# Plain fp32 products in place of split products in the output projection of a state-space attention part

## What is computed

```
proj = h @ W_in.T                       # gate (4096), hidden (4096), B and C (128 each), dt (64)
hidden, B, C = silu(conv4(...))         # causal convolution of 4 taps per channel, then silu
y = (chunked scan of C, B, dt*hidden) + D * hidden          # 64 heads of 64 channels, chunks of 32 tokens
yf = y * silu(gate)
yn = norm_w * (yf * rsqrt(mean(yf*yf) + 1e-5))
return yn @ W_out.T                     # 4096 -> 256: the output projection
```

## Time and profile before

| | us |
|---|---|
| median of 3 runs | 2118.07 |
| the three runs | 2114.32, 2118.07, 2148.47 |
| span of the profiled execution | 2145.4 |
| PE, DVE, ACT, POOL busy over the span | 1740.8, 1467.5, 1005.9, 1011.7 |

### The profile page before, as it was taken

How to read it: one execution, slowest core, us unless ns; L and a number is a source line. 1 busy time by engine, 2 the same in 40 slices (tenths; PEclk the granted TensorE clock), 3 DMA queues, 4 the chain that set the end, 5 groups by cost and what they waited for, 6 DMA issues and landing times. The chain is left out here.

```text
span 2145.4 us, 36030 instructions
## 1 busy us (share of the span) xinstructions
PE 1740.8 (81%) x9416; PEld 1471.1 (69%) x9416; DVE 1467.5 (68%) x2219; ACT 1005.9 (47%) x1824; POOL 1011.7 (47%) x938
## 2 busy tenths in 40 slices
PE   6699996899987999968999888604999999999400
PEld 5577775677775777756777666403999998999300
DVE  3589996699985899966999845512544556554344
ACT  3555553655554555536555432202655666555100
POOL 0445553455543455535555403885433444333576
PEclk8899998999998999989999966857555667555555
DMA  3022220122210222201222101224766777666233
GB/s 120 0 70 83 77 82 21 38 74 83 81 57 0 75 78 83 76 21 42 78 75 83 45 0 63 81 86 136 228 195 205 231 235 245 198 198 203 89 118 103
DMA packets 110563, 217.46 MB, mean 101 GB/s; under 512 B 14160, under 2 KB 51536, under 8 KB 110416
## 3 DMA queue, kind: packets, MB, share of 16 engines
q1 hardware_dynamic: 94928, 171.07, 25.2%
q0 software_dynamic: 15616, 46.15, 6.7%
HBM read 160.55 MB, written 56.62 MB: 101 GB/s over the span
## 5 line engine op out<-in xcount | busy, mean ns | idle before, releaser
L965 DVE SCALAR_TENSOR_TENSOR e<-bank,scal,e 128x511 f32<-128x511 f32 (+2 forms) x384 | 284.0, 740 | 36.6 <-DVE e L965 18.2
L436 PEld LDWEIGHTS bank<-m,xt 128*128 128x128 f32 x2048 | 243.4, 195 | 84.0 <-DVE xt L1006 83.8
L1288 POOL TENSOR_TENSOR ew_lo<-ew,ew_hi 128x352 fp32r<-128x352 f32 x160 | 152.4, 953 | 309.1 <-ACT ew_hi L695 309.1
L436 PE MATMUL bank<-m,xt 128*128 128x128 f32 x2048 | 267.6, 285 | 30.0 <-DVE xt L1006 29.7
L1301 POOL TENSOR_TENSOR ssq<-ssq,ysq 128x512 f32<-128x512 f32 x128 | 164.0, 1281 | 227.3 <-ACT ysq L753 227.3
L1288 POOL TENSOR_TENSOR wi_lo<-wi,wi_hi 128x512 fp32r<-128x512 f32 x128 | 219.2, 1713 | 51.3 <-ACT wi_hi L695 51.3
L368 PE MATMUL bank<-h_hi,wi_hi 128*128 x512 | 227.6, 445 | 17.0 <-POOL wi_lo L1288 14.6
L760 ACT ACTIVATE e<-e 128x512 f32<-128x512 f32 x128 | 81.0, 633 | 324.2 <-DVE e L965 324.1
L878 DVE TENSOR_TENSOR hid_lo_rows<-hid_rows,hid_hi_rows 88x256 fp32r<-88x256 f32 x160 | 67.4, 421 | 231.8 <-ACT hid_hi_rows L695 231.8
L368 PE MATMUL bank<-hw_hi,ew_hi 128*88 128x128 f32 x640 | 220.1, 345 | 0.4 <-POOL ew_lo L1288 0.2
L1000 DVE TENSOR_TENSOR m<-el,gmask 128x1024 f32<-128x1024 f32 x128 | 219.8, 1717 | 0.1
(11 more groups left out here) (247 smaller groups left out, 4436.4 us busy)
## 6 DMA issues: line engine op xcount, KB each, us to landing
ew<-expert_w SPq DMA_DIRECT2D x160, 432.0 KB, 3.8
wi<-in_w SPq DMA_DIRECT2D x128, 256.0 KB, 2.5
grouped<-zeros_out SPq DMA_DIRECT2D x64, 320.0 KB, 2.3
x_rows<-grouped POOLq DMA_DIRECT2D x80, 256.0 KB, 4.4
outputs<-y_rows SPq DMA_DIRECT2D x80, 256.0 KB, 4.4
wo<-out_w SPq DMA_DIRECT2D x128, 128.0 KB, 2.0
x_all<-x_t SPq DMA_DIRECT2D x4, 512.0 KB, 8.3
out_t<-x_all SPq DMA_DIRECT2D x4, 512.0 KB, 3.5
```

What stands on the lines that cost most here:

```text
L436: i = mm(p_y[:, t * P:(t + 1) * P], xt[:, t, hd * HEAD_DIM:hd * HEAD_DIM + P], m[:, t, hd, :], start=hd == 0, stop=hd == 1)
L965: v.scalar_tensor_tensor(dst[:, d:], src[:, 0:SEQ - d], taps(TAPS - 1 - d), dst[:, d:], ALU.mult, ALU.add).then_inc(S[done], 1)
L1288: return g_.tensor_tensor(dst, src, hi.bitcast(F32), ALU.subtract)
```

## The change

The output projection multiplies y itself with weights that carry the norm's weight, `wn = wo * norm_w`, in plain fp32. y_hi, y_lo, wo_hi and wo_lo with their instructions and semaphores are gone; wn stands where wo_hi stood on ACT. Since y is now read by PE itself, DVE waits before it overwrites a half of y until the out group that read it is done.

```diff
-            wo_hi = sb("wo_hi", [P, 2, EMB], F32R, on=part)
-            wo_lo = sb("wo_lo", [P, 2, EMB], F32R, on=part)
+            wn = sb("wn", [P, 2, EMB], on=part)
...
             def load_out(b, j, par):
-                sp.wait_ge(S["wo_lo"], START["wo_lo"] + b * PAIRS + j - 1)
+                sp.wait_ge(S["wn"], START["wn"] + b * PAIRS + j - 1)
...
                 if do_out:
-                    pe.wait_ge(S["y_lo"], g - 1)
-                    pe.wait_ge(S["wo_lo"], START["wo_lo"] + g - 1)
+                    pe.wait_ge(S["y_done"], START["y_done"] + g - 1)
+                    pe.wait_ge(S["wn"], START["wn"] + g - 1)
                     for k in range(KE):
-                        w = slice(k * P, (k + 1) * P)
-                        i = split_mm(p_out[k][:, :], wo_hi[:, par, w], wo_lo[:, par, w], y_hi[:, par, :], y_lo[:, par, :],
-                                     do_out == "first", do_out == "last")
+                        i = mm(p_out[k][:, :], wn[:, par, k * P:(k + 1) * P], y[:, par, :],
+                               start=do_out == "first", stop=do_out == "last")
...
-                if finish:
-                    act.wait_ge(S["y_done"], START["y_done"] + g - 1)
-                    act.wait_ge(S["out_mm"], START["out_mm"] + g - 3)
-                    f(y_hi[:, par, :], y[:, par, :], ACT.Identity, scale=scal[:, bass.ds(j - 2, 1), NW_AT:NW_AT + 1]
-                      .rearrange("p a n -> p (a n)")).then_inc(S["y_hi"], 1)
...
                 if finish:
+                    act.wait_ge(S["y_done"], START["y_done"] + g - 1)
                     act.wait_ge(S["ssq_done"], START["ssq_done"] + g - 2)
...
-                    high(wo_hi[:, q, :], wo[:, q, :]).then_inc(S["wo_hi"], 1)
+                    f(wn[:, q, :], wo[:, q, :], ACT.Identity, scale=scal[:, bass.ds(j - 1, 1), NW_AT:NW_AT + 1]
+                      .rearrange("p a n -> p (a n)")).then_inc(S["wn"], 1)
...
-                if finish:
-                    dve.wait_ge(S["y_hi"], START["y_hi"] + g - 1)
-                    dve.wait_ge(S["out_mm"], START["out_mm"] + g - 3)
-                    v.scalar_tensor_tensor(y_lo[:, par, :], y[:, par, :], col(j - 2, NW_AT), y_hi[:, par, :].bitcast(F32),
-                                           ALU.mult, ALU.subtract).then_inc(S["y_lo"], 1)
...
                     dve.wait_ge(S["y_sq"], START["y_sq"] + g - 2)
+                    dve.wait_ge(S["out_mm"], START["out_mm"] + g - 2)
                     v.tensor_tensor(y[:, q, :], yt[:, :], gs[:, q, :], ALU.mult).then_inc(S["y_done"], 1)
...
-                if take_out:
-                    pool.wait_ge(S["wo_hi"], g)
-                    low(wo_lo[:, 1 - par, :], wo[:, 1 - par, :], wo_hi[:, 1 - par, :]).then_inc(S["wo_lo"], 1)
```

More of the change, by code:

```diff
@@ L75, in sem @@
             return ctx.enter_context(nc.semaphore(name))
-        START = {"wi_lo": 2, "wo_lo": 2, "gate": 2, "y_done": 2, "out_mm": 2, "y_sq": 2, "y_hi": 2, "attn_res": 1,
+        START = {"wi_lo": 2, "wn": 2, "gate": 2, "y_done": 2, "out_mm": 2, "y_sq": 2, "attn_res": 1,
                  "taps": 1, "silu_g": 1, "xt_done": 1, "y_skip": 1, "ssq_done": 1, "ssm": 1,
@@ L231, in program @@
             ssq = sb("ssq", [P, SEQ], on=part)
-            acc, xf, gs, y, y_hi, y_lo = (a[:, n, :].rearrange("p (q n) -> p q n", q=2) for a, n in
-                                          ((e1, 0), (e1, 1), (e2, 0), (e2, 1), (mov_hi, 0), (mov_lo, 0)))
+            acc, xf, gs, y = (a[:, n, :].rearrange("p (q n) -> p q n", q=2) for a, n in
+                              ((e1, 0), (e1, 1), (e2, 0), (e2, 1)))
             attn, ms, rms, rinv, rinv_diag = bcacc, z[:, 0:TILES], zabs[:, 0:TILES], zln[:, 0:TILES], zexp[:, :]
@@ L259, in program @@
             bc_mm bc_tap0 bc_taps bc_silu g_mm g_done mov_hi mov_lo seg_mm seg_exp seg_done
-            wi0 wi1 wo0 wo1 wi_hi wi_lo wo_hi wo_lo
-            hid gate tap0 taps silu_x silu_g turned xt_done m_done ssm y_skip y_done y_sq y_hi y_lo
+            wi0 wi1 wo0 wo1 wi_hi wi_lo wn
+            hid gate tap0 taps silu_x silu_g turned xt_done m_done ssm y_skip y_done y_sq
             out_mm ssq_done ssq_zero ssq_mm ssq_var ssq_std ssq_inv ssq_wide rinv_mm attn_scaled attn_res
@@ L1293, in take_in, with slot @@
                 low(wi_lo[:, par, :], wi[:, par, :], wi_hi[:, par, :]).then_inc(S["wi_lo"], 1)
-            def slot(b, j, par, next_in=True, take_out=True, finish=True):
+            def slot(b, j, par, next_in=True, finish=True):
                 g = b * PAIRS + j
@@ L1328, in _ @@
                 take_in(b, 0, 0)
-                slot(b, 0, 0, take_out=False, finish=False)
+                slot(b, 0, 0, finish=False)
                 slot(b, 1, 1, finish=False)
@@ L1336, in _ @@
                 slot(b, PAIRS, 0, next_in=False)
-                slot(b, PAIRS + 1, 1, next_in=False, take_out=False)
+                slot(b, PAIRS + 1, 1, next_in=False)
             def pass_by():
```

## The result

The change made the kernel faster. The first measurement gave a median of 2078.46 us (2064.16 to 2108.98) against 2133.27 us of the kernel before: ratio 0.972, 95% interval 0.965 to 0.978. A ratio compares the fast runs of both kernels only, while the medians are over all runs, so it isn't quite their quotient. I had also given 0.85 to a change within 2% and 0.12 to what the first measurement shows, faster by over 2%.

What follows compares the result with a forecast made beforehand. DVE was taken to bound the 7.07 us slot, PE after it at 6.97: 2.9 us a sequence in the loop plus 1.9 at its end, times 4 sequences, 19 us off the 2118.07 us median: 2099 us, range 2068 to 2131.

Steps and rivals of the forecast that it cites:

- DVE sets the pace by 0.4 us: Head-pair loop before: DVE fills the 7.07 us slot, PE works 6.66 us and waits 0.4 us for DVE.
- 0.4 us, that is all the room there is: Head-pair loop: PE's waits for DVE, 0.4 us a slot in two places, were taken as all that could be gained.
- The forecast of 6.1 us of work: DVE's slot after the change: 7.07 less 1.17 for y_lo plus 0.22 for tap 2 waiting on tap 1.
- 1.85 + 1.49 + 1.83 + 1.80 = 6.97: PE's slot after the change in us: hid with the turning, gate, ssm, out; PE sets the pace.
- Rival C: PE's groups in the loop cost less than their rows: slot 6.77 us, 43 us off, 2075 us; chance 0.12.
- first-record price: On PE, the first record of a group of products was taken to cost 0.1 us more than the others.
- POOL "nothing": POOL loses wo_lo and keeps its 1.75 us wi_lo, which isn't late for the next hid: no effect on time.
- Forecast 1.9 us a sequence: End of each sequence's pair loop: 0.9 us at slot 31's yt plus 1.0 us in the last slot's chain.
- The last chain: Last slot, from yt to the sum of squares on PE: 4.64 us falls to 3.6, a gain of 1.0 us.
- The step from the last slot but one to the last: End of a sequence: without y_lo, DVE takes yt at once after slot 31's ssm, gaining 0.9 us.
- A: Before ssm, PE still waits for xt: slot 7.29 us, 18 us slower in all, 2136 us; chance 0.12.
- B: The plain out group takes 1.90 us in the loop: slot stays 7.07, only 7.6 us gained, 2110; chance 0.1.

Runs made afterwards that it cites:

- e8: Kernel before with y_lo moved on DVE from behind tap 1 to between m and xt, nothing left out: slot 6.77 us, loops 911.2 us.
- e2: Kernel before without wo_lo on POOL, PE reading wo_hi in its place: slot 7.07 us, loops 937.3 us.
- e1: Kernel before without y_lo on DVE, PE still making six split products with y_hi in its place: slot 6.36 us, loops 852.0 us.
- e11: Kernel before, split products kept, y_lo made by POOL, norm weight put into the weights on ACT: slot 6.39 us, timed ratio 0.957 to before.
- e4: Changed kernel with an operation like wo_lo put back on POOL, result unused: slot 6.72 us, loops 884.6 us.
- e3: Changed kernel with an operation like y_lo put back on DVE between taps 1 and 2, result unused: slot 6.85 us, loops 907.4 us.
- e7: Kernel before with POOL adding only 8 of the square's 512 columns: slot 7.42 us, loops 980.9 us.

## Why the prediction was right, and where it was wrong

**What sets the pace before.** "DVE sets the pace by 0.4 us" was wrong. DVE was in the ring but its list was not the bound: e8 runs the same list in 6.77 us, e2 shortens one entry with no effect. The step that failed was to take a DVE share of 97.4% without a named wait for work. That PE would take over was right: 100% busy and no wait in the profile after.

**The room on PE.** "0.4 us, that is all the room there is" was wrong too: with no wait left, PE runs the very same products in 6.36 us (e1) or 6.39 (e11), so there was 0.7 us. The waits for xt and for tap 3 were read rightly as waits, but each costs 0.1 us more than its gap, which went into the groups as work. And there was a third. y_lo ends at 251.25 and out starts at 251.30, too short a wait for its row to name. The last record of ssm there is

```profile
251.25 0.28 PE L436 MATMUL bank<-m,xt 128*128 128x128 f32 x1
```

and out's second record comes 0.38 us behind it (0.40 in the median of the loops), where e1 and e8, in which y_lo is not wanted or ready long before, have 0.345. From the last record before a group to the group's second, the three waits cost 0.44 (xt), 0.17 (tap 3) and 0.05 us (y_lo) a slot.

**DVE's part.** The forecast of 6.1 us of work is too high, since m takes 1.2 us and not 1.68. From start to start, one slot of DVE after is 0.61 for xt, 2.57 for the taps, 0.78 for yt, 0.66 for y and about 1.2 for m: 5.8. The 0.22 us for tap 2 behind tap 1 was right: 0.88 from one tap to the next was forecast, and three taps of 0.75 take 2.53 us in one piece. Nothing of it mattered, as the slot was PE's.

**PE's slot, the term that was mis-sized.** I summed 1.85 + 1.49 + 1.83 + 1.80 = 6.97; measured 1.74 + 1.47 + 1.79 + 1.72 = 6.72. hid and ssm were read behind a wait and brought its 0.1 us along, though the waits were to go; out was read from a group with 0.08 us more in its first record; gate was taken from an out that had waited for y_lo. That is 0.25 us a slot, 0.25 x 29 x 4 = 29 us of the 39 missing. Rival C came nearest, with 6.77 us a slot and 43 us, and its argument, that some of the first-record price could be the end of a wait, was the right one. I gave it 0.12, since out paid the price with no wait in its row; the wait was y_lo's. The estimate that I had set aside, 1.73 us from the 215.7 ns of the Trainium skill (TensorE: Matmul & The Clock Gate, section "Wait — 56ns, not 53.3ns?"), is near what the plain group took: 1.72. The split products take 0.23 us each and not 215.7 ns.

**POOL "nothing".** Right for the slot (e4), for a wrong reason: POOL's operations stretch DVE's m and y_lo, which only didn't matter once PE set the pace.

**The ends.** Forecast 1.9 us a sequence, measured (58.1 - 0.35 x 29 x 4) / 4 = 4.4. The last chain was right (1.1 against 1.0). The step from the last slot but one to the last, for which I had 0.9, gave 1.8 (7.2 on the mean before, 5.35 after). m is 0.5 us shorter there, and in the first sequence ssm took 2.05 us where before it took 3.58:

```profile
341.12 3.58 PE L436 MATMUL bank<-m,xt 128*128 128x128 f32 x16 [2.33 <-DVE xt L1006]
```

It came after a wait of 2.33 us, and the mean granted clock from 342.0 to 344.8 us was 0.58, so part of it ran at the lower of the two levels; in the changed kernel the clock is 1.00 there, after a wait of 1.25 us.

Missing from my sum was the step into slot 2, from the first y to the second: 7.14 before, 5.57 after, 1.6 us. Leaving out y_lo alone brings it to 6.11 (e1).

**Rivals.** A did not come: PE has no named wait ahead of ssm in the loop's rows. B did not come: 1.72 in the loop. The time, 2078, lay inside the range of 2068 to 2131 because I had widened it for C and for the spread of the runs; the gain itself was three times the forecast. In the same measurement the kernel before took 2133 us and not the 2118 that I started from, so that the sum would have given 2114. That the number was as near as 20 us owes something to luck.

## What to carry to other kernels

A DVE operation with two SBUF inputs that runs beside a POOL operation can hide a wait, as y_lo did (0.74 us alone, 1.26 in the loop): compare its duration with the shortest instance of the same shape before its busy share is read as work, and follow the ring over all engines. Before an operation is taken off, look whether moving it in the order or to another engine does the same: e8 took 0.30 us of a slot by order alone, e11 0.68, the change 0.35. When a sum for PE is put together from groups, read each group where it stands behind no wait. Its first record can be drawn early; from the last record before the group to its second, nothing is hidden.

## What the runs showed of the hardware that I had not expected

Plain fp32 with 512 columns costs PE 0.43 us a record and 0.86 a product at the full clock, three split fp32r products 0.23 each, 0.70: splitting is the faster form here by 0.32 us for two products (1.72 against 1.40). The held y_lo, or its like, ends 0.54 to 0.56 us after the POOL operation that held it in each of the 116 slots of the loops, in four kernels (before, e2, e3, e7). And less work on POOL made the kernel 41 us slower in its loops (e7).
